# Scores of two successive units sent back to back on TensorE in two conditioned attentions

## What is computed

```
xn = ln(x, g_norm)
q = (xn @ Wq) split into 16 heads of 64;  k, v = xn @ Wkv (one head of 64 each)
k, v get one null key and value in front
q = l2norm(q) * q_scale;  k = l2norm(k) * k_scale
sim = q k^T * 8 + bias[i - j]          (a table of relative positions per head)
sim = -big where the key lies after the query, or where the mask is off
out = softmax(sim) v;  result = ln(out @ Wout, g_out)
```

## Time and profile before

| | |
|---|---|
| three runs, us | 2733.27, 2728.49, 2728.35; median 2728.49 |
| profiled execution, span | 2726.8 us (the page gives no other time of this execution) |
| TensorE matmul, busy | 2616.0 us, 96% of the span |
| VectorE, ScalarE, GpSimd, busy | 1438.6, 1060.3, 914.2 us |
| mean granted TensorE clock | 0.979 |

### The profile page before, as it was taken

The page is one execution under the profiler, slowest core; times in us unless marked ns, Lnnn a source line. Parts: engine busy times, 40 slices in busy tenths (PEclk is TensorE's granted clock), DMA queues, the critical chain, the costliest instruction groups (busy, mean ns, idle before and its releaser), DMA issues. The chain is left out here.

```text
span 2726.8 us, 37423 instructions
## 1 busy us (share of the span) xinstructions
PE 2616.0 (96%) x13249; PEld 1547.9 (57%) x13249; DVE 1438.6 (53%) x3343; ACT 1060.3 (39%) x2587; POOL 914.2 (34%) x953
## 2 busy tenths in 40 slices
PE   7999998999999899999999999999999899899998
PEld 4565555533443448658658568556555566544456
DVE  7466565467776343243342333555655577555545
ACT  4767675344544111121121121265656455212122
POOL 3656564177777023102102012575655300000000
PEclk9999999889999899999999999999999999999998
DMA  4000000000000510000000010332323000400000
GB/s 156 1 1 1 1 1 20 12 12 13 13 11 7 179 54 1 1 1 1 0 1 1 0 42 1 107 117 88 120 84 112 19 1 1 128 0 2 2 10 26
DMA packets 82622, 91.94 MB, mean 34 GB/s; under 512 B 14982, under 2 KB 66063, under 8 KB 82312
## 3 DMA queue, kind: packets, MB, share of 16 engines
q1 hardware_dynamic: 82120, 89.04, 10.5%
q0 software_dynamic: 320, 0.52, 0.1%
HBM read 83.19 MB, written 2.14 MB: 31 GB/s over the span
## 5 line engine op out<-in xcount | busy, mean ns | idle before, releaser
L1011 POOL TENSOR_TENSOR cb_sc<-cb_toep,cb_mk 128x128 f32<-128x128 f32 (+3 forms) x256 | 216.1, 873 | 190.4 <-ACT cb_pr L1049 179.5
L1011 POOL TENSOR_TENSOR cb_bias<-cb_bias,cb_mk 128x128 f32<-128x128 f32 (+3 forms) x256 | 214.9, 869 | 147.9 <-DMA cb_bias<-in_fside_16xSxS 147.8
L1647 DVE TENSOR_REDUCE gb_bmax<-PS 128x8 f32<-128x512 f32 x256 | 164.5, 684 | 88.4 <-PE PS L1425 87.6
L398 PE MATMUL PS<-ident,cb_pr 128*128 128x128 f32 x1280 | 198.2, 284 | 4.0 <-ACT cb_pr L1049 2.3
L699 DVE CUSTOM_DVE_ANT_0 cb_sc<-PS,cb_sc,cb_sneg 128x128 f32<-128x128 f32 (+3 forms) x256 | 129.8, 546 | 124.6 <-PE PS L388 121.1
L3300 POOL TENSOR_TENSOR eb_S<-ff_h 128x1024 f32<-128x1024 f32 x16 | 38.0, 2377 | 464.2 <-PE PS L2220 464.1
L398 PEld LDWEIGHTS PS<-ident,cb_pr 128*128 128x128 f32 x1280 | 135.0, 141 | 96.2 <-issue 82.0
L1806 ACT ACTIVATE gb_pt<-PS 128x512 f32<-128x512 f32 x256 | 139.6, 596 | 110.8 <-PE PS L1432 105.6
L1055 ACT ACTIVATE cb_pt<-PS 128x128 f32<-128x128 f32 (+3 forms) x448 | 163.7, 415 | 38.3 <-PE PS L398 37.9
L1425 PE MATMUL PS<-gb_ks,gb_qs 32*128 32x512 f32 x512 | 170.9, 668 | 7.8 <-DVE gb_bmax L1647 6.7
L699 DVE CUSTOM_DVE_ANT_0 cb_bias<-PS,cb_bias,cb_sneg 128x128 f32<-128x128 f32 (+3 forms) x256 | 129.3, 546 | 92.0 <-PE PS L388 91.1
(11 more groups left out here) (557 smaller groups left out, 5091.2 us busy)
## 6 DMA issues: line engine op xcount, KB each, us to landing
cb_bias<-in_fside_16xSxS SPq DMA_DIRECT2D x64, 256.0 KB, 2.9
cb_bias<-in_fside_16xSxS SPq DMA_DIRECT2D x64, 192.0 KB, 2.5
ff_h<-in_L_ffn_h_w SPq DMA_DIRECT2D x2, 4096.0 KB, 22.8
cb_bias<-in_fside_16xSxS SPq DMA_DIRECT2D x64, 128.0 KB, 2.2
cb_toep<-rel_table SPq DMA_DIRECT2D x8, 512.0 KB, 6.2
cb_bias<-in_fside_16xSxS SPq DMA_DIRECT2D x64, 64.0 KB, 2.3
ff_w<-in_L_ffn_w_w SPq DMA_DIRECT2D x3, 1024.0 KB, 8.2
gb_ks<-ga_room SPq DMA_DIRECT2D x64, 32.0 KB, 2.0
```

The costliest lines, as they stand in the source:

```text
L398: ins = pe.transpose(PS[:, bank, j * P:j * P + P], pr[:, v % 2, e, j * P:j * P + P], ident)
L1011: ins = pool.tensor_tensor(biases(v, e), turned(h, n) if L0 else biases(v, e), mk[:, b % 2, packed(t):packed(t) + n], ALU.add)
L1647: dve.tensor_reduce(bmax[:, n % 2, t, g + e, 0:NB], PS[:, bank + e, :].rearrange("p (n k) -> p n k", k=64), AX.X, ALU.max)\
```

## The change

Only the order in which TensorE sends the scores changes. Before, unit v + 2's scores go out ahead of the transposes of every unit v. After, they go out at odd v alone, two units at a time: v + 2 and v + 3. At t = 1 these are t = 3 of this head pair and t = 0 of the next; at t = 3 they are t = 1 and t = 2 of the next. At v = 0 unit 2 is sent by itself. The programs of the other engines, the semaphores' counts and the PSUM banks stay as they are.

```diff
--- before.py
+++ after.py
@@ -531,8 +531,12 @@
             for v in range(N):
                 b, u, m, t = at(v)
                 last, more = b > 0, b + 1 < B
-                if v + 2 < N:
-                    scores(v + 2)
+                if v == 0:
+                    scores(2)
+                elif v % 2:
+                    for ahead in (v + 2, v + 3):
+                        if ahead < N:
+                            scores(ahead)
                 if t == 0 and v:
                     values(*divmod(v // NT - 1, MC))
                 turn(v)
```

## The result

The changed kernel takes 2743.66 us (median of 7 runs, 2734.73 to 2751.53), the kernel before 2729.72 us (7 runs, 2728.25 to 2734.74). The ratio is 1.0046, with a 95% interval of 1.003 to 1.0062. That is 14 us more, over the upper end of the predicted range, 2738.

What follows compares the result with a forecast made beforehand. TensorE, busy 96% of 2726.8 us, was taken as the bound. Cycle classes of -10.4, -1.8, 0 and +10.6 us net -1.6; with 1.7 us around the span, 2727 us, own range 2723 to 2733, 8-in-10 range 2716 to 2738.

Steps and rivals of the forecast that it cites:

- TensorE's saving: Joined scores and transposes in both attentions: 0.575 us less fixed cost per cycle, 35.6 us over 62 if nothing else happened.
- ScalarE's chain in plain cycles: Eight cycles with nothing mixed in: ScalarE's copies and exponentials set when the values matmuls start, so change 0.
- The 27 cycles: Cycles with VectorE work before the next t = 0 minimum, or TensorE work mid-cycle only: +10.6 us together.
- The 9 with little after T3: Cycles with 0.3 to 0.9 us of TensorE work after the last transposes: -0.1 to -0.4 each, -1.8 us.
- the covered class: 18 cycles with projection or query matmuls after the last transposes: the full 0.575 us saved each, -10.4 us.
- first head pair of a batch: Seven cycles, six with VectorE's row sums before the next t = 0 minimum: 0 to +0.8 each, 3.0 us.
- The price of 0.75 us: Per-cycle cost of VectorE's late minimum for the next t = 0, upper bound for the 27 cycles: 20 us.
- V uncovered: Values matmuls wait for the last copies to SBUF, 0.9 to 1.2 us in some 35 cycles, some 30 us.
- (d): Slower: VectorE's late minimum for the next t = 0 stalls the second scores pair, 0.75 us a cycle; about 2736, chance 0.23.
- (a): Whole kernel: no measurable change, gains in covered cycles given back elsewhere; the forecast itself, 2727 us, chance 0.50.
- (b): Whole kernel faster: new waits mostly fall where TensorE waits already; 2716 to 2722 us, centre 2719, chance 0.24.
- (c): Whole kernel faster by far: counted fixed parts alone, 62 x 0.575, give 2693 us; chance 0.03.

Runs made afterwards that it cites:

- the first pair alone: Kernel before, with only the scores of t = 3 and the next head pair's t = 0 sent together: 2725.79 us, ratio 0.9982 to the kernel before.
- the second alone: Kernel before, with only the scores of the next head pair's t = 1 and t = 2 sent together: 2754.64 us, ratio 1.0078 to the kernel before.
- second execution: Both kernels profiled once more, unaltered: the changed kernel 2737.84 us, the kernel before 2733.28 us.
- the combined kernel: Kernel before, first scores pair joined everywhere, second in chosen head pairs, VectorE's masked minimum for the next t = 0 earlier in chosen places: 2717.37 us, ratio 0.9958.
- The selective kernel: Kernel before, first scores pair joined everywhere, second only in chosen head pairs, VectorE's order unaltered: 2726.16 us, ratio 0.9989 to the kernel before.
- the kernel that took two thirds of V's waits away: Changed kernel, with the next head pair's first transposes sent ahead of the values matmuls: 2741.38 us, ratio 1.0038 to the kernel before.
- the experiment that moves D(0'): Changed kernel, with VectorE's masked minimum for the next t = 0 ahead of mixed-in work only where it was late: 2733.15 us, ratio 1.0012 to the kernel before.

## Why the prediction was wrong, step by step

**TensorE's saving: right.** 0.365 and 0.21 us a cycle were claimed, 0.575 together. The TensorE-bound cycles, 21.56 to 21.01 and 13.21 to 12.65, show 0.55. Of these the first pair alone gives 0.35 (21.21, 12.85) and the second alone 0.20 (21.36). The drain rule of the Trainium skill (TensorEngine Tiling (Array Packing), Key Properties), taken alone at 0.3 us, is short of it. In the trace of the cycle of the earlier trace rows the step from one block's last start to the next block's first is 0.09 to 0.10 us longer than between two matmuls of that width in a row. The change removes three such steps a cycle, 0.3 us. The rest lies behind the first start of a block, with which its first weight load begins (within 0.01 us; later ones begin ahead of their matmul): 0.10 to 0.11 us more to the next start in a block of scores, 0.05 in a block of transposes. Two of the one and one of the other make 0.27 us.

**ScalarE's chain in plain cycles: right.** Eight cycles, 70.00 us before and 69.97 after, 0 predicted.

**The failed step: "18 cycles with a projection or a query matmul group after T3 ... so V is never short of M(3): the full 0.575 each, -10.4 us."** They gave +0.04 (-1.0 in the second execution of the changed kernel, which has no half clock there). That V finds its copies was true in most of them, and it was not the question. I asked which wait ends last before V, and not what hangs on the blocks that S2' now goes ahead of, nor which other engine sets the cycle. There are four cases.

The third head pair (6 cycles) gave -0.2 each, but +1.0 in one with half clock. The first pair alone gives nothing there (138.64 against 138.21 in the table). The output projection reads VectorE's product of the spread (L693), and starts 0.05 us behind the product's first half in both kernels; what TensorE saves ahead of it turns into a wait:

```profile
299.24 3.72 PE L421 MATMUL PS<-ca_wo,cb_QT 128*128 128x256 f32 x16 [0.29 <-DVE cb_QT L693]
```

The fourth gave -0.55 in four, those bound by TensorE throughout, and 0.0 and +0.19 in two of the second attention. There VectorE has the output's statistics ahead of D(1') and M(3). VectorE, then TensorE, in the changed kernel:

```profile
1911.15 1.39 DVE L728 BATCH_NORM_STATS2 cb_ost<-cb_ob 128x6 f32<-128x256 f32 x4
...
1914.49 0.68 DVE L710 COPY cb_pt<-PS 128x512 f32<-128x512 f32 x1
```

```profile
1915.31 2.38 PE L410 MATMUL PS<-cb_pt,cb_kv 128*64 128x512 f32 x16 [0.79 <-DVE cb_pt L710]
```

V waits 0.79 us for M(3), although four matmuls of line 338 (1.88 us) stand between T3 and V: the cover was there, and was not enough. In the kernel before V waits 0.23 us in this place.

The fifth gave -0.33 and -0.56 in the first batch of each attention. In the next two batches of the first attention it gave +0.64 each. Its T2 waits 0.87 us for X2. ScalarE and TensorE in the changed kernel:

```profile
217.85 0.60 ACT L1030 ACTIVATE cb_sq<-PS 128x512 f32<-128x512 f32 x1 [0.93 <-PE PS L338]
...
218.95 1.28 ACT L1081 ACT_TABLE_LOAD   x1
...
220.47 1.28 ACT L1053 ACT_TABLE_LOAD   x1
221.76 0.51 ACT L1053 ACTIVATE cb_pr<-cb_sc,cb_nm 128x256 f32<-128x256 f32 x1
```

```profile
225.38 0.52 PE L398 MATMUL PS<-ident,cb_pr 128*128 128x128 f32 x3 [0.87 <-ACT cb_pr L1053]
```

The last queries (the L338 group of 215.93 above) are copied by ScalarE, then come two table loads of 1.28 us with a square root between, then the exponentials for T1 and T2. This chain starts at the queries, and S2' stands ahead of them now: 0.64 us of columns, +0.64 us in the cycle (15.18 to 15.82). With S2' of the cycle before kept behind the queries the combined kernel is back at 15.18:

```profile
218.76 0.66 PE L398 MATMUL PS<-ident,cb_pr 128*128 128x128 f32 x4
...
219.88 0.52 PE L398 MATMUL PS<-ident,cb_pr 128*128 128x128 f32 x3
```

T2 follows there with no wait for X2. The selective kernel, which kept that pair, has 16.02. So this case is shown by undoing it.

In the next two batches of the second attention it gave +0.85 each, which is D(0') late after all, in a cycle that I had held for covered. All engines in the changed kernel:

```profile
2031.25 2.75 DVE L739 TENSOR_SCALAR cb_ob<-cb_ob,cb_omv,cb_orstd 128x256 f32<-128x256 f32 x4
...
2031.66 2.19 POOL L1015 TENSOR_TENSOR cb_bias<-cb_bias,cb_mk 128x384 f32<-128x384 f32 x2 [2.12 <-DMA cb_bias<-in_fside_16xSxS]
...
2034.33 1.18 PE L388 MATMUL PS<-cb_kT,cb_QT 64*128 64x384 f32 x4 [0.87 <-DVE cb_nm L703]
```

The output normalisation stands between D(3) and D(0') as in the earlier trace rows, and takes 2.75 us, twice the 1.38 of that row, while GpSimd works. The trace of the kernel before has this price in this very place:

```profile
2012.46 2.75 DVE L735 TENSOR_SCALAR cb_ob<-cb_ob,cb_omv,cb_orstd 128x256 f32<-128x256 f32 x4
```

I took the row of the last batch, where GpSimd is idle beside it. With D(0') moved ahead of it these cycles are at 12.65 us (13.21 before, 14.05 after): the full gain.

**The 27 cycles: mechanism right, size too small. The 9 with little after T3: wrong in sign.** Together +8.8 us was predicted and +18.5 measured (17.8 in the table and 0.7 in the two first cycles, with nothing net in the other two classes). Sorted by what stands behind T3, the 27 gave about +17 where +10.6 was forecast. The 9 gave about +1.4 in place of -1.8, by +0.28 in each of the three eighth head pairs of the first attention, +0.2 in its three sixth ones and +0.7 in its very first cycle, while its and the other attention's second head pair of the last batch gave the -0.36 each that was forecast. So of the 20 us between the forecast -1.6 and the measured +18.5, 10.4 are the covered class, some 6.5 the 27 and some 3 the 9.

By position some of the 27 held: third of the first batch +0.5 (0.4 predicted), seventh of the first attention +1.2 (1.1), second head pair +2.3 over eight cycles (2.7 over six), sixth +2.3 over eight (1.6 over five). The fourth and fifth of the last batch came to +1.0 (1.8 predicted) by luck: the two fourth ones fell by 1.5 us where +0.4 was forecast, the two fifth ones grew by 2.4 where it was +1.4, one of them the very cycle of the earlier trace rows (+1.3, and +0.9 in the second executions, for the +0.7 worked out from it). The mis-sized term is "first head pair of a batch ... 3.0 us", which measured +10.5 over eight cycles, and +8.1 in the second executions. Of the +10.5, 5.2 us is one cycle, 9.30 to 14.50 (10.15 and 12.43 in the second executions). VectorE and GpSimd, then TensorE, and its windows, in the changed kernel:

```profile
1854.85 1.04 DVE L722 TENSOR_TENSOR cb_cpn<-cb_rden,cb_pn 128x64 f32<-128x64 f32 x1
1855.81 1.09 DVE L671 COPY cb_rd<-cb_rden 128x64 f32<-128x64 f32 x2
...
1854.82 1.94 POOL L1015 TENSOR_TENSOR cb_bias<-cb_bias,cb_mk 128x384 f32<-128x384 f32 x2 [0.67 <-DMA cb_bias<-in_fside_16xSxS]
...
1857.23 1.75 PE L388 MATMUL PS<-cb_kT,cb_QT 64*128 64x384 f32 x4 [2.69 <-DVE cb_nm L703]
1858.91 1.97 PE L398 MATMUL PS<-ident,cb_pr 128*128 128x128 f32 x8
```

```profile
1853.00:1857.00 4.00, 1.54 (x7) 0.59 (x4) 3.93 (x10) 2.27 (x6) 3.09 (x4) 1.00 0.58 176
1857.00:1861.00 4.00, 3.77 (x14) 2.70 (x15) 2.00 (x10) 1.82 (x7) 2.85 (x3) 0.59 0.25 85
```

and the same work of VectorE in the kernel before:

```profile
1841.90 0.23 DVE L718 TENSOR_TENSOR cb_cpn<-cb_rden,cb_pn 128x64 f32<-128x64 f32 x1
1842.04 0.29 DVE L667 COPY cb_rd<-cb_rden 128x64 f32<-128x64 f32 x2
```

The last steps of the row sums meet GpSimd's 1.94 us and take four times as long; S2' waits 2.69 us; then the clock falls to its lower level and T3 takes 1.97 us in place of 1.09. The price of 0.75 us, read from a row in which VectorE had GpSimd idle beside it, was a lower bound and I used it as the upper one. No run keeps GpSimd away from the row sums, so how much of the 5.2 us is GpSimd, how much the order and how much the clock is read from these rows and not tested.

One reading of the prediction was off besides: in the first attention the 3.0 us before V are half of TensorE's waits, 5.9 us, not nearly all. No term rests on it.

**V uncovered: right in the trace, and not the cause.** 45 waits, 31.2 us, close to the 30 in some 35 cycles that were forecast. But the kernel that took two thirds of V's waits away gained nothing, and the plain cycles carry 0.93 us of it at no cost.

**The signs of being wrong.** None of the three that the prediction named came up: plain cycles stayed, the joined blocks are 0.2 us shorter each, and the waits sum to 46.7 us, between 30 and 60. They tested the savings and the amount of waiting. None looked at the length of the covered cycles other than the one of the earlier trace rows, which is bound by TensorE.

**The rivals.** (d), slower by D(0') late, was nearest: its mechanism makes up 12 to 14 us of the 13 to 18 by the experiment that moves D(0'). Its count fell short by the contended price, and by the cycles counted as covered. Its chance of 0.23 was too low, because the -10.4 us of the covered class stood against it as a certainty. (a) fell with that class. (b) held for half of the change: the first pair alone is 4.3 us faster in the cycles. (c) held for none.

**What stays open.** Of the 13 to 18 us, the part that half clock adds is not separated. It is some 1.2 us in one cycle (20.39 against 19.19 for its twin) and part of the 5.2 in the other, and it came in the kernel before too. Why the eighth head pair of the first attention grows by 0.28 us was read from the trace only and not tested by itself, other than by undoing the second pair (36.83 us with the first pair alone, as before). Why cycles of the second attention differ by up to 0.9 us between executions of one kernel is open too.

## What to carry to other kernels

Moving a block of work earlier to save its fixed cost (0.2 us here) delays all that it overtakes by its full length (0.64 us); where a chain through another engine starts at an overtaken block, that is the price, and whether the engine itself finds cover later does not matter. Ask of each repeat of the pattern which engine's chain sets it, and join only where TensorE itself does: here joining the second pair only in chosen head pairs, with VectorE's order changed in step, turned +0.46% into -0.42%. Price a wait with the duration that the blocking work has when its neighbours run, look for that duration at every place where the work recurs, and do not take a sum of waits for what their removal is worth.

## What the runs showed that was not expected

- **VectorE beside GpSimd.** The same four instructions, 128 x 256 in fp32, took 1.38 us with GpSimd idle and 2.75 us beside it, a 128 x 64 product 0.23 and 1.04 us, two 128 x 64 copies 0.29 and 1.09 to 2.23 us. The Trainium skill (SBUF — State Buffer, Who interferes with whom) says that VectorE and GpSimd share a pair of ports, which copies and tensor-scalar forms in a two-port mode and forms with two inputs in SBUF have to wait for. These rows agree in which instructions grew, and each grown one ends 0.05 to 0.16 us behind the end of a GpSimd instruction (the product of 1.04 us at 1855.89, GpSimd at 1855.81); they do not show who held the port. So a change of order that moves a normalisation of VectorE under GpSimd's work cost 1.4 us here, with no instruction added.
- **The granted clock falls inside a busy stage.** The mean granted clock of both attentions rounds to 0.99 or 1.00, and still stretches at the lower level occur and last 3.4 us each, a few 6.8. Those shown above came right behind waits of TensorE of 1.57, 2.69 and 3.64 us; the one from 467.3 in the kernel before came behind a wait of 0.88 us. Three (from 181.8 us in the changed kernel, from 1870.2 in the kernel before and from 1987.0 in the second-pair kernel) came with no wait right before, behind the 1.85 us of sixteen matmuls of 16 columns each. V takes 3.97 to 4.20 us then, not 2.38. Most waits bring none. Kernels with the second pair everywhere had two to five such stretches, those with the first pair alone or with chosen pairs none; but two fell in one execution of the kernel before.
- **Cycles repeat.** In the first attention of the two executions of the changed kernel seven of the eight head-pair sums agree within 0.02 us, and the third head pair's differs by one stretch at half clock (1.2 us), while their spans differ by 7 us. There, effects of 0.1 us could be read from single traces, where 12 timed runs gave an interval of 0.35% in width. In the second attention, which reads its bias from memory, cycles of one kernel differed by up to 0.9 us, and a second trace was needed.
